# Two cross-attention layers: the norms' square root in four pieces, the product PM shared by VectorE and GpSimd, and its row sums moved from GpSimd to TensorE

## The reference

```python
q = heads(hidden_states @ W_q); k_t = heads(text_ehs @ W_k); v_t = heads(text_ehs @ W_v)
probs_t = softmax(einsum('bhsd,bhtd->bhst', q, k_t) * attn_scale)
text_out = einsum('bhst,bhtd->bhsd', probs_t, v_t)
attn_scores = einsum('bhsd,bhnd->bhsn', q, k_ip) * attn_scale
qsem = l2norm(einsum('bhst,bte->bhse', probs_t, text_ehs))
sem = einsum('bhse,bne->bhsn', qsem, l2norm(ip_ehs))
probs_ip = softmax(attn_scores + SEM_SCALE * sem) * spatial_mask
out = (text_out + einsum('bhsn,bhnd->bhsd', probs_ip, v_ip)) @ W_out + b_out + residual
```

## Time and profile before

| | us |
|---|---|
| median of 3 runs | 1898.73 (1897.92 to 1899.94) |
| profiled execution | 1902.26 |
| its span | 1900.3 |
| TensorE busy | 1664.9 (88%) |
| VectorE busy | 1459.4 (77%) |
| ScalarE busy | 1033.4 (54%) |
| GpSimd busy | 861.0 (45%) |

### The profile page before, as it was taken

One profiled execution on the slowest core, in us unless ns is written; L12 is line 12 of the kernel. 1 busy time (PEld: TensorE's weight loads), 2 busy tenths in 40 slices (PEclk: granted clock), 3 DMA queues, 4 the chain that ended last, 5 costly groups with the idle time before them and its releaser, 6 DMA issues.

```text
span 1900.3 us, 42137 instructions
## 1 busy us (share of the span) xinstructions
PE 1664.9 (88%) x14344; PEld 1460.7 (77%) x14344; DVE 1459.4 (77%) x3732; ACT 1033.4 (54%) x2188; POOL 861.0 (45%) x666
## 2 busy tenths in 40 slices
PE   5999999999999998479888988988898898889875
PEld 4888888888888886368777877877787787778764
DVE  4677777777777786458887987987797897879784
ACT  3466666666666665236555555655554565555452
POOL 4232332333332322455556455555655555564553
PEclk9899999999999999689899988988998898899898
DMA  6334444444444432533133223312322331231201
GB/s 169 101 106 122 118 120 121 117 123 114 120 118 112 124 102 60 166 94 87 45 79 97 61 67 83 88 56 75 97 62 67 83 89 52 79 96 53 57 21 35
DMA packets 186491, 172.64 MB, mean 91 GB/s; under 512 B 25884, under 2 KB 186282, under 8 KB 186282
## 3 DMA queue, kind: packets, MB, share of 16 engines
q1 hardware_dynamic: 186282, 169.97, 32.5%
HBM read 110.19 MB, written 57.59 MB: 88 GB/s over the span
## 4 chain that ended last, share of the span: by engine, by line
PE 37%; POOL 9%; DVE 8%; issue 3%; ACT 1%; SPq 1%; DMA 0%; DVEq 0%; POOLq 0%; ACTq 0%
PE MISC L60 12%; PE GP L60 11%; POOL NRM L1238 6%; PE NAT L735 3%; PE TR L756 3%; DVE PM L1076 3%; PE PV L786 3%; DVE ZP L1070 2%; POOL ZS L1220 1%; PE PV L789 1%; PE PV L746 1%; PE MISC L885 1%; PE MISC L824 1%; PE MISC L806 1%; DVE NRM L1095 1%
## 5 line engine op out<-in xcount | busy, mean ns | idle before, releaser
L1220 POOL TENSOR_TENSOR ZS<-ZP 128x256 f32<-128x256 f32 x320 | 322.6, 1008 | 422.2 <-DVE ZP L1070 422.2
L60 PE MATMUL GP<-PH,GH 128*128 128x256 f32 (+1 forms) x960 | 257.8, 296 | 129.7 <-DVE ZP L1070 129.4
L314 ACT ACTIVATE P<-TA 128x512 f32<-128x512 f32 x320 | 202.0, 632 | 254.5 <-DVE TA L460 253.9
L60 PEld LDWEIGHTS GP<-PH,GH 128*128 128x128 f32 (+1 forms) x960 | 187.9, 196 | 140.6 <-issue 131.7
L1076 DVE SCALAR_TENSOR_TENSOR PM<-P,PH 128x512 f32<-128x512 f32 x320 | 291.3, 910 | 0.0
L1070 DVE TENSOR_TENSOR ZP<-GP,PM 128x512 f32<-128x512 f32 x320 | 219.2, 685 | 58.5 <-PE GP L60 53.0
L60 PE MATMUL GP<-PH,GL 128*128 128x256 f32 (+1 forms) x960 | 250.4, 288 | 0.0
L445 DVE TENSOR_REDUCE MX<-NAT 128x2 f32<-128x154 f32 x320 | 101.7, 318 | 172.4 <-PE NAT L142 170.4
L1062 DVE TENSOR_REDUCE MX<-NAT 128x2 f32<-128x504 f32 x320 | 214.8, 672 | 11.4 <-PE NAT L735 10.5
L460 DVE TENSOR_TENSOR TA<-TR,ST 128x512 f32<-128x512 f32 x320 | 219.0, 685 | 3.0 <-PE TR L162 2.8
L932 ACT ACTIVATE P<-TR 128x512 f32<-128x512 f32 x320 | 190.3, 595 | 45.4 <-PE TR L756 41.5
(11 more groups left out here) (229 smaller groups left out, 4371.9 us busy)
## 6 DMA issues: line engine op xcount, KB each, us to landing
QS<-qk_parts SPq DMA_DIRECT2D x480, 64.0 KB, 2.7
qk_parts<-PARTS SPq DMA_DIRECT2D x96, 224.0 KB, 2.7
CT<-in_ctx_t SPq DMA_DIRECT2D x32, 512.0 KB, 4.3
KS<-qk_parts SPq DMA_DIRECT2D x240, 64.0 KB, 2.7
KS<-qk_parts SPq DMA_DIRECT2D x240, 63.0 KB, 2.9
qk_parts<-PARTS SPq DMA_DIRECT2D x48, 192.0 KB, 2.2
QS<-NH SPq DMA_DIRECT2D x480, 4.0 KB
qk_parts<-PARTS SPq DMA_DIRECT2D x32, 220.5 KB, 4.0
```

Of the source, the lines that this page charges most:

```text
L60: ins = e.matmul(out, lhs, rhs, start=(n == 0), stop=(n == len(pairs) - 1))
L314: e.activation(P[:, s % NP, :], TA[:, s % 2, :], ACT.Exp, scale=SCALE).then_inc(q["exp"], 1)
L1220: e.tensor_tensor(ZS[:, s % NZ, :], ZP[:, s % 2, 0:S], ZP[:, s % 2, S:2 * S], ALU.add).then_inc(q["zs"], 1)
```

## The change

PM becomes P - PH with PH now half of P (`mul` by 0.5), so that both PH and PM are half of what they were, and E21's column is 4 instead of 1 to make up for it. VectorE computes the first half of PM (keys 0 to 127) and GpSimd the second, with a semaphore `pm_q` of its own, on which ZP waits. ZS is gone: ZP has five buffers, and TensorE sums both halves, with eight matmuls with E21 for a group instead of four. PV and PVS move from `HG + 3` to `HG + 2`. The root is taken in four pieces of 128x10 elements on steps 46 to 49, and `sem`, `fu`, `tx` and `ptt`, `ipm` move back by three steps, `hst` by two.

```diff
@@ -657,9 +657,10 @@
...
     AT = dict(q=(-3, 1, 5), k=(-2, 2, 6), spill=(-1, 3, 7), x_in=-22, xts=-12, c_in=-18, cts=-6, gr=(4, 8), v=(10, 12), kbd=12, scm=14,
-              vip_in=20, vip=26, cmb=46, sem=(47, 48, 49), fu=50, tx=(51, 52, 53), ptt=53, ipm=56, hst=60, om=(69, 73), out=75, xb_in=59, xb=63)
+              vip_in=20, vip=26, cmb=46, root=(46, 47, 48, 49), sem=(50, 51, 52), fu=53, tx=(54, 55, 56), ptt=56, ipm=59, hst=62, om=(69, 73), out=75,
+              xb_in=59, xb=63)
     ONCE = -12
-    NS, NZ, NIP = 4, 6, B * NI
+    NS, NZ, NIP = 4, 5, B * NI
 
@@ -680,7 +681,7 @@
...
     PH, PM = sb("PH", [128, NS, 2 * S], F32R), sb("PM", [128, 2, 2 * S])
-    ZP, ZS = sb("ZP", [128, 2, 2 * S]), sb("ZS", [128, NZ, S])
+    ZP = sb("ZP", [128, NZ, 2 * S])
     GH, GL = sb("GH", [128, 2, 3, 128], F32R), sb("GL", [128, 2, 3, 128], F32R)
@@ -699,13 +700,13 @@
...
                    "stack4 mrow0 mrow1 store fill clear clear_q w_hi w_lo xt_hi xt_lo ct_hi ct_lo qk qk_f qk_hi qk_lo gr vc gh gl w_ip once once_s once_q rn "
-                   "vall_out vip_in kbd scm sc vip vm v nat mx mxt nh nm tr exp ph pm gp zp zs pv pvs ont on cmb nrm fu fexp tx "
+                   "vall_out vip_in kbd scm sc vip vm v nat mx mxt nh nm tr exp ph pm gp zp pm_q pv pvs ont on cmb nrm fu fexp tx "
                    "ptt pt ipm hs hst ht_hi ht_lo om y xb")
...
     ki_raw = stage(ON[:, :, :, :].rearrange("p b a n -> p (b a n)"), 0, KC)
-    vi_raw = stage(ZS[:, :, :].rearrange("p r n -> p (r n)"), 0, KC)
+    vi_raw = stage(ZP[:, :, :].rearrange("p r n -> p (r n)"), 0, KC)
     once = XB[:, :, :].rearrange("p a n -> p (a n)")
@@ -769,7 +770,7 @@
...
                                             (GL[0:N2, p, 2, :], p1)]).then_inc(q["gp"], 1)
-            g = due_group(t, HG + 3)
+            g = due_group(t, HG + 2)
             if g is not None:
@@ -780,13 +781,15 @@
...
                 e.wait_ge(q["nm"], min(g + 4, B * NGRP))
-                e.wait_ge(q["zs"], HG * g + HG)
+                e.wait_ge(q["zp"], HG * g + HG)
                 for i in range(2):
...
                                  start=i == 0, stop=False)
-                for j, h, r in heads:
-                    ins = e.matmul(PV[SLOT * j:SLOT * (j + 1), 0:S], E21[:, :], ZS[:, (HG * g + j) % NZ, :], start=False, stop=True)
+                for i in range(2):
+                    for j, h, r in heads:
+                        ins = e.matmul(PV[SLOT * j:SLOT * (j + 1), 0:S], E21[:, :], ZP[:, (HG * g + j) % NZ, i * S:(i + 1) * S],
+                                       start=False, stop=i == 1)
                 ins.then_inc(q["pv"], 1)
@@ -933,8 +936,8 @@
...
                 e.wait_ge(q["exp"], s + 1)
-                e.copy(PH[:, s % NS, :], P[:, s % NP, :]).then_inc(q["ph"], 1)
-            g = due_group(t, HG + 3)
+                e.mul(PH[:, s % NS, :], P[:, s % NP, :], 0.5).then_inc(q["ph"], 1)
+            g = due_group(t, HG + 2)
             if g is not None:
@@ -1048,7 +1051,7 @@
...
         e.wait_ge(q["fill"], 7)
-        e.memset(E21[:, 21:22], 1.0).then_inc(q["fill"], 1)
+        e.memset(E21[:, 21:22], 4.0).then_inc(q["fill"], 1)
         e.memset(VB[:, :, 0, :, D:D + 1], 1.0).then_inc(q["fill"], 1)
@@ -1063,18 +1066,20 @@
...
             if 0 <= s < B * H:
-                if s >= 2:
-                    e.wait_ge(q["zs"], s - 1)
+                if s >= NZ:
+                    e.wait_ge(q["pv"], (s - NZ) // HG + 1)
                 e.wait_ge(q["pm"], s + 1)
+                e.wait_ge(q["pm_q"], s + 1)
                 e.wait_ge(q["gp"], s + 1)
-                e.tensor_tensor(ZP[:, s % 2, :], GP[:, :], PM[:, s % 2, :], ALU.mult).then_inc(q["zp"], 1)
+                if s == 0:
+                    e.wait_ge(q["once"], 2)
+                e.tensor_tensor(ZP[:, s % NZ, :], GP[:, :], PM[:, s % 2, :], ALU.mult).then_inc(q["zp"], 1)
             s = t - 1
...
                 e.wait_ge(q["ph"], s + 1)
-                e.scalar_tensor_tensor(PM[:, s % 2, :], P[:, s % NP, :], 2.0, PH[:, s % NS, :].bitcast(F32), ALU.mult,
-                                       ALU.subtract).then_inc(q["pm"], 1)
+                e.tensor_tensor(PM[:, s % 2, 0:S], P[:, s % NP, 0:S], PH[:, s % NS, 0:S].bitcast(F32), ALU.subtract).then_inc(q["pm"], 1)
             g = due_group(t, HG - LEAD + 1)
@@ -1083,14 +1088,14 @@
...
                     e.wait_ge(q["tx"], b)
-                    e.wait_ge(q["nrm"], b)
+                    e.wait_ge(q["nrm"], 4 * b)
                 e.wait_ge(q["on"], NGRP * (b + 1))
...
             if b is not None:
-                e.wait_ge(q["nrm"], b + 1)
+                e.wait_ge(q["nrm"], 4 * b + 4)
                 e.wait_ge(q["cmb"], 6 * b + 2)
@@ -1210,14 +1215,14 @@
...
         for t in range(T0, T1):
-            s = t - 2
+            s = t - 1
             if 0 <= s < B * H:
                 if s == 0:
-                    e.wait_ge(q["once"], 2)
-                if s >= NZ:
-                    e.wait_ge(q["pv"], (s - NZ) // HG + 1)
-                e.wait_ge(q["zp"], s + 1)
-                e.tensor_tensor(ZS[:, s % NZ, :], ZP[:, s % 2, 0:S], ZP[:, s % 2, S:2 * S], ALU.add).then_inc(q["zs"], 1)
+                    e.wait_ge(q["w_lo"], 4)
+                if s >= 2:
+                    e.wait_ge(q["zp"], s - 1)
+                e.wait_ge(q["ph"], s + 1)
+                e.tensor_tensor(PM[:, s % 2, S:2 * S], P[:, s % NP, S:2 * S], PH[:, s % NS, S:2 * S].bitcast(F32), ALU.subtract).then_inc(q["pm_q"], 1)
             for m, off in enumerate(AT["k"]):
@@ -1228,15 +1233,17 @@
...
                 e.tensor_tensor(XB[:, :, :], XB[:, :, :], BIAS[:, :].unsqueeze(1).broadcast_to([128, 2, C]), ALU.add).then_inc(q["xb"], 1)
-            b = due(t, AT["cmb"])
-            if b is not None:
-                if b == 0:
-                    e.wait_ge(q["fill"], FILLS)
-                else:
-                    e.wait_ge(q["cmb"], 6 * b)
-                e.wait_ge(q["cmb"], 6 * b + 2)
-                e.tensor_tensor(NRM[:, 1, :, :].rearrange("p a h -> p (a h)"), NRM[:, 0, :, :].rearrange("p a h -> p (a h)"), HALF[:, 0:2 * H],
-                                ALU.pow).then_inc(q["nrm"], 1)
+            for n, off in enumerate(AT["root"]):
+                b = due(t, off)
+                if b is not None:
+                    i, h0 = n // 2, n % 2 * (H // 2)
+                    if n == 0:
+                        if b == 0:
+                            e.wait_ge(q["fill"], FILLS)
+                        else:
+                            e.wait_ge(q["cmb"], 6 * b)
+                        e.wait_ge(q["cmb"], 6 * b + 2)
+                    e.tensor_tensor(NRM[:, 1, i, h0:h0 + H // 2], NRM[:, 0, i, h0:h0 + H // 2], HALF[:, 0:H // 2], ALU.pow).then_inc(q["nrm"], 1)
             for c in range(3):
```

## The result

The changed kernel takes 2114.8 us (median of 4 runs, 2105.3 to 2128.1) where the kernel before takes 1899.3: 11.4% slower, ratio 1.1135 with a 95% interval of 1.1094 to 1.1176. Forecast were 2057 us and slower. The profiled execution is the slowest of the four (2128.1 us, mean granted clock 0.929; the others have 0.936 to 0.939), so what is read from its trace is a little more than what the medians differ by: 226 us where the medians say 215.

What follows compares the result with a forecast made beforehand. TensorE, 88% busy, was taken as the bound, idling behind the square root's gap. Terms summed to +9.5 us a period, +142 over 15 periods, +159 with first batch and end, giving 2057 us against the median; range 1960 to 2135.

Steps and rivals of the forecast that it cites:

- PV's wait: PV at HG+2 waits on TensorE for VectorE's NH behind ZP and PM: 5 x 1.65 = +8.2 us a period.
- Empty steps: Six of a batch's steps r0 to r19 have nothing after GP, exposing the GP-ZP loop: 6 x 0.7 = +4.2 us.
- E21: Four more TensorE matmuls per group, covered by nothing: 5 x 0.43 = +2.2 us a period.
- The root in four: Quarter roots of 2.0 us on GpSimd remove VectorE's gap: 7.4 idle and 2.5 low clock, -9.9 us a period.
- the queue's cost: GpSimd's queue around r6, with root quarters and half of PM, delays ZP and GP: +3.9 us, bounds 2.9 and 8.2.
- hst: At step 62, TensorE waits about 1.1 us for a MISC bank and next ZP slips 0.5: +1.6 us a period.
- The clock: TensorE's low clock of 2.5 us a period goes with the root's gap; empty-step waits were said to cost no clock.
- the one that it kept for a miss: Sign: if the clock falls in every batch between r6 and r10, 2 us a period are missing from the sum.
- Rival A: Busy GpSimd in r6 to r10 holds VectorE's PM halves at the SBUF port: 75 us more, 2132; chance 0.18.
- Rival B: The waits overlap, so the empty steps and r6 cost half: 60 us less, 1997; chance 0.20.
- D: The split does not split: every quarter root on GpSimd costs the whole 6.8 us, 2312 us; chance 0.03.
- Rival C: Faster: PV's wait hardly there as NH is ready before GP ends, empty steps covered too: 1859 us; chance 0.07.

Runs made afterwards that it cites:

- e3: The changed kernel with the low part of NH (L1086) moved on VectorE from behind PM to ahead of ZP: 1952.8 us.
- e4: The changed kernel with PV and PVS back at HG+3 and six ZP buffers: 1907.6 us, ratio 1.0036.
- e1: The kernel before with the root in four pieces and the change's whole shifted table, ZS, PM and PV as before: 1890.8 us, ratio 0.994.
- e8: The changed kernel with the four root instructions as multiplications of the same shape, so the output lacks the square root: 2021.1 us.
- e11: The changed kernel with all of PM on VectorE, PV still at HG+2: 2098.7 us.
- e6: The kernel before with PV and PVS at HG+2 and nothing else: 2314.1 us, 21.8% slower.
- e5: e1 with root pieces at 47, 50, 51, 52, sem at 53, 54, 54, and ptt, ipm, hst later: 1846.1 us, ratio 0.9721.
- e7: e4 with the root pieces and the rest of the table as in e5: 1838.1 us.
- e12: The kernel before with root at 46, 47, 50, 51, sem 52 to 54, ipm 60, hst 63, VIP's mask at 29: 1824.6 us, ratio 0.9594.

## Why the prediction was right, and where it was short

The sign, the waits and the range held; the clock did not. The measured growth is 215 us where the working said 159. Per period it said +9.5; the traces say +14.6. By its own steps:

- *PV's wait.* Predicted 5 x 1.65. Measured 1.74 to 1.76 on average in four of the five steps, and 2.42 in r10: 9.4 a period. Right, and e3 shows that it causes the loss. Moving PV costs 13.5 us a period in all (after against e4), near the 12.4 of the two terms for it, but partly by luck: 2.9 of the 13.5 is the lower clock, which neither term held.
- *Empty steps.* Predicted 0.7 each; the step behind r11, r12, takes 3.69 us where it took 3.06 before, with 0.50 of wait in it. Right.
- *E21.* Predicted 0.43 a group; e4 against e1 gives 0.43.
- *The root in four.* Quarters predicted at 2.0 us, measured 1996 ns. That 64 and 40 elements give the price of 10 was sound. GP of r9 was to come 2.3 us later, and waits 2.26. But the queue's cost as a whole was predicted at 3.9 and is 6.4 by e8: 2.5 of waits, the rest the lower clock.
- *hst.* The wait was predicted at 1.1 and is 0.88. `ptt` in r16 waits 0.5 for VectorE's FU, which no term had.
- *The clock.* This is the step that failed. The sum took 2.5 us a period for half clock away with the gap, and put nothing in its place, since "waits of this size cost no clock": the earlier trace rows show a clock of 1.00 with waits of half a microsecond in each step. PV's wait is three times that. The 2.5 was right for the kernel before (2.5 are lost there), but the changed kernel loses 6.3. The sum in those terms: forecast were waits +9.8 (restarts in them), E21 +2.2, clock -2.5; measured are waits +7.9, E21 +2.15, clock +3.8, and 0.8 that is left over. The waits were even somewhat less than forecast, and the 6.3 us by which the clock is off are more than the whole miss of 5.1.

The signs that the prediction named came for the most part: 49 waits of PV for NH in 1000 to 1800 us, quarters of 2.0 us, no 6 us wait for the root, hst's wait for PARTS. One did not: GP waited for ZP 67 times, not well over 100. And the one that it kept for a miss came too: it said that 2 us a period would be missing if the clock fell in every batch between r6 and r10. It fell there in all 14, and 3.5 us of the 6.3 are lost in r9 and r10.

Rival A, the port: with the root's cost gone and the split kept (e8), r9 and r10 got 5.7 us shorter; with the split gone too, all of PM on VectorE (e11), 5.9. So nearly all of it was GpSimd's queue with the root in it. VectorE's PM halves took 0.59 us on average (0.41 alone, the longest 2.2), 3.5 us a period in all. Contention is there, but no run shows the 5 us on the path that A put on top. That the measured 2115 lies nearer to A's 2132 than to 2057 does not speak for it, as the clock makes up the difference. Rival B is refuted by the empty steps, which cost what was forecast, and D by the quarters. Rival C named the place from which the sign turns, PV's wait: with it almost gone the change is at 1.027 (e3), with PV at its old step at 1.0036 (e4).

Of the 2.26 us of wait in r9, 0.51 are left without the root's cost (e8). How much of that difference is the length of the queue and how much the order in which its pieces got the port was not separated.

## What to carry to other kernels

When a consumer is moved a step earlier, read the order on every engine in that step and ask what it waits for that was a step old until now; here a semaphore that PV had never had to wait for became TensorE's largest wait, and moving one 0.4 us instruction ahead took 162 us off. A gap on an engine that works in order is gained only if the work that made it also fits in the steps into which it is spread: count that engine's microseconds per step first (15.6 in 10.8 here). In a kernel bound by TensorE, price the waits with the clock behind them: a row with shorter waits does not show it, and even waits of nearly the same length cost between 2.2 and 6.3 us a period here, so give the term a range of its own.

## What the hardware showed that was not expected

The lower clock is not a matter of long gaps only. One gap of 7.4 us in a period (before) cost 2.5 us by it; five waits of 1.74 to 2.4 and smaller ones between (after) cost 6.3; five of 2.0 to 2.1, with none longer than 2.4 in the 14 periods (e11), 6.8; and waits of 2.0 to 2.1 together with the gap (e6) 14.9, at a mean clock of 0.81. Without the root's cost (e8) PV's waits were 1.74 us on average in four steps and 1.77 in the fifth, yet only 2.2 us were lost, at a mean of 0.97. The share of PV steps with a clock below 1.00 in the 3 us from PV's start goes the same way: 8 of 70 in e8, 25 in the changed kernel, 36 in e11, 50 in e6. So it is not the length of the single wait alone that decides, and these runs do not show the rule.

A short VectorE instruction with two SBUF inputs was held beside a long GpSimd one in three kernels (FU beside CTSL in e5, e7 and e12). In e5 it took 2.29 to 2.31 us in 13 of 16 batches and ended 0.18 us after CTSL each time. In the last three, with no CTSL beside it, it took 0.33 us. The Trainium skill, "SBUF — State Buffer", section "Who interferes with whom", says that such an instruction and a GpSimd one that reads SBUF exclude each other for a whole instruction; by that rule, the traces agree.
